# Three Mamba blocks inside one decoder kernel: the skip as a matmul, the gate product on VectorE, one SiLU pass for gate and u

## The reference, cut to what matters

```python
xz = jnp.einsum('bld,ed->ble', h, inproj)
xc, z = jnp.split(xz, 2, axis=-1)
xc = jax.nn.silu(causal_conv(xc, convw, convb))
xdbl = jnp.einsum('ble,fe->blf', xc, xproj)
dt = jax.nn.softplus(jnp.einsum('blr,er->ble', xdbl[..., :R], dtw) + dtb)
A = -jnp.exp(Alog)
# one step of ssm_scan: h = exp(dt*A) * h + (dt*x) * B;  y = sum over 16 states of h * C
y = ssm_scan(dt, Bm, Cm, xc, A) + xc * Dp
y = y * jax.nn.silu(z)
return jnp.einsum('ble,de->bld', y, outproj)
```

## Time and profile before

| | us |
|---|---|
| three runs, median (lowest to highest) | 2925.25 (2921.18 to 2925.6) |
| profiled execution: span from first to last instruction | 2927.1 |
| TensorE busy, of the span | 2456.1 (84%) |
| VectorE busy | 1872.1 (64%) |
| ScalarE busy | 1332.9 (46%) |
| GpSimd busy | 1530.9 (52%) |

### The profile page before, as it was taken

One profiled execution on the slowest core, in us unless ns is written; L12 is line 12 of the kernel. 1 busy time (PEld: TensorE's weight loads), 2 busy tenths in 40 slices (PEclk: granted clock), 3 DMA queues, 4 the chain that ended last, 5 costly groups with the idle time before them and its releaser, 6 DMA issues. The chain is left out here.

```text
span 2927.1 us, 26112 instructions
## 1 busy us (share of the span) xinstructions
PE 2456.1 (84%) x8044; PEld 1106.1 (38%) x8044; DVE 1872.1 (64%) x2521; ACT 1332.9 (46%) x2087; POOL 1530.9 (52%) x1340
## 2 busy tenths in 40 slices
PE   7989989889897788688888549999588989778978
PEld 3333323333332233333333338888332333223322
DVE  2999999999999933466663400000239999994334
ACT  4656466565664433345555212222056565542333
POOL 2999999999999811500000230000439999982010
PEclk9999999999999999899999669999689999999989
DMA  4031230321203000612310324444230320300000
GB/s 186 1 115 47 94 117 1 122 70 55 115 1 115 0 21 17 141 24 33 45 23 1 138 106 181 177 175 175 79 155 1 116 94 24 115 1 20 0 9 29
DMA packets 72193, 215.12 MB, mean 73 GB/s; under 512 B 14044, under 2 KB 39271, under 8 KB 53495
## 3 DMA queue, kind: packets, MB, share of 16 engines
q1 hardware_dynamic: 65380, 180.85, 18.9%
q10 hardware_dynamic: 3602, 24.22, 2.5%
q0 software_dynamic: 3072, 8.39, 0.9%
HBM read 187.80 MB, written 25.43 MB: 73 GB/s over the span
## 5 line engine op out<-in xcount | busy, mean ns | idle before, releaser
L895 POOL TENSOR_TENSOR s_dbu<-s_dx,s_bc 128x512 f32<-128x512 f32 x768 | 967.8, 1284 | 47.9 <-DVE s_psum L561 44.1
L480 PE MATMUL s_psum<-s_hc,ident 128*128 128x512 f32 x1536 | 832.2, 632 | 181.2 <-DVE s_hc L581 170.2
L764 ACT ACTIVATE s_psum<-s_dt,s_a_neg 128x512 f32<-128x512 f32 x768 | 521.6, 688 | 590.5 <-DVE s_hc L581 589.5
L480 PEld LDWEIGHTS s_psum<-s_hc,ident 128*128 128x128 f32 x1536 | 257.9, 192 | 695.2 <-DVE s_hc L581 505.4
L581 DVE TENSOR_TENSOR s_hc<-s_psum,s_bc 128x512 f32<-128x512 f32 x624 | 419.8, 673 | 0.6 <-PE s_psum L480 0.4
L561 DVE TENSOR_TENSOR_SCAN s_psum<-s_psum,s_state,s_dbu 128x512 f32<-128x512 f32 x312 | 395.1, 1277 | 18.5 <-ACT s_psum L764 12.7
L561 DVE TENSOR_TENSOR_SCAN s_psum<-s_psum,s_dbu 128x512 f32<-128x512 f32 x312 | 381.3, 1222 | 22.0 <-ACT s_psum L764 13.8
L1968 ACT ACTIVATE s_probs<-s_banks 128x512 f32<-128x512 f32 (+3 forms) x384 | 169.2, 493 | 149.5 <-PE s_banks L1693 107.0
L2381 POOL DMA_INDIRECT s_rows_in<-moe_out_rows,s_place x32 | 30.6, 957 | 357.0 <-DMA moe_out_rows<-s_ys 347.5
L2360 ACT ACTIVATE s_hidden<-s_banks,s_w 128x256 f32<-128x256 f32 x184 | 77.1, 470 | 300.9 <-PE s_banks L2183 300.9
L163 POOL TENSOR_TENSOR s_pair<-s_res 128x512 f32<-128x512 f32 x4 | 5.0, 1265 | 386.1 <-issue 384.6
(11 more groups left out here) (306 smaller groups left out, 3320.6 us busy)
## 6 DMA issues: line engine op xcount, KB each, us to landing
s_bc<-fwd_rows SPq DMA_DIRECT2D x64, 1024.0 KB, 4.7
s_bc<-m_rows SPq DMA_DIRECT2D x32, 1024.0 KB, 4.7
s_w<-in_moe_w SPq DMA_DIRECT2D x23, 1028.0 KB, 7.2
s_w<-in_moe_w ACTq DMA_DIRECT2D x23, 1024.0 KB, 5.5
qk_parts<-s_parts SPq DMA_DIRECT2D x48, 128.0 KB, 1.9
s_stack_q<-qk_parts SPq DMA_DIRECT2D x48, 128.0 KB, 4.5
s_stack_k<-qk_parts SPq DMA_DIRECT2D x48, 128.0 KB, 7.6
moe_in_rows<-s_zero SPq DMA_DIRECT2D x1, 5888.0 KB, 18.8
```

Source lines behind the costliest of these rows:

```text
L480: pe.matmul(psum[:, SCANS + block_no % 2, :], consts["ident"][:], hc[:, unit % PRODUCTS, :], start=(n == 0), stop=(n == NS - 1)).then_inc( ...
L764: act.activation(psum[:, unit % SCANS, :], dt[:, g % 2, i // NS, :], ACT.Exp, scale=a_neg[CHUNKS[g][0]][:, i:i + 1]).then_inc(decay_ready, 1)
L895: pool.tensor_tensor(dbu[:, unit % TERMS, :], dx[:, g % 2, i // NS, :], bc[:, 2 * n, :], ALU.mult)\
```

## The change

1. The skip is a matmul: `make_skip` (GpSimd) makes diag(D) for each block, and `total` adds skip_in times u as the first matmul of a block's sums, four more per chunk.
2. `skip` and GpSimd's `times_gate` go. VectorE's new `times_gate` reads the sums from PSUM, multiplies by the gate and writes dx, at unit 12 of the next block (the skip stood at unit 3).
3. The gate of a chunk is projected earlier: `in_z` blocks 0, 1, 2 in units 30, 46 and 62 of the chunk before, block 3 in units 16 and 17 of the chunk itself, ahead of `out`, which now begins at 18. ScalarE stores them at units 36 and 51, and 3 and 22. At unit 23 one stretch does SiLU on the gate and on the next u.
4. GpSimd weighs 15 units, i % 16 in (2, 6, 8, 12, 14) of the first three blocks, from two `hs` buffers.
5. Softplus is made in two halves, `dt` has six buffers, and the slots of `rows`, `steps_of`, `var`, `add_res`, `scale_y`, relu and times_u move by one to three units. The table of work banks follows the new order. At the head of each stage the four gate blocks of chunk 0 are projected and copied from PSUM by VectorE (`keep_gate`) between its relu sums.

```diff
-LENT = [i < 3 * NS and i % 4 == 2 for i in range(UNITS)]
+LENT = [i < 3 * NS and i % NS in (2, 6, 8, 12, 14) for i in range(UNITS)]
+GATED, STEPS = 12, 6
-        dt = s.sb("dt", [P, 2, EB, CH])
+        dt = s.sb("dt", [P, STEPS, CH])
-        hs = s.sb("hs", [P, CH])
+        hs = s.sb("hs", [P, 2, CH])
+        skip_in = s.sb("skip_in", [P, EB, P])
...
                 unit = g * UNITS + i
                 block_no, n = unit // NS, unit % NS
                 if n == 0 and block_no >= 2:
-                    pe.wait_ge(y_read, block_no - 1)
+                    pe.wait_ge(y_ready, block_no - 1)
                 elif n == 0:
                     pe.wait_ge(ln_log, block_no + 3)
+                if i == 0:
+                    pe.wait_ge(skip_made, (CHUNKS[g][0] + 1) * EB)
+                if n == 0:
+                    pe.matmul(psum[:, SCANS + block_no % 2, :], skip_in[:, i // NS, :],
+                              u[:, g % 2, i // NS, :], start=True, stop=False)
                 if LENT[i]:
                     pe.wait_ge(product_lent, lent(unit + 1))
                 else:
                     pe.wait_ge(product_ready, own(unit + 1))
                 pe.matmul(psum[:, SCANS + block_no % 2, :], consts["ident"][:], hc[:, unit % PRODUCTS, :],
-                          start=(n == 0), stop=(n == NS - 1)).then_inc(product_used, 1)
+                          start=False, stop=(n == NS - 1)).then_inc(product_used, 1)
...
             variance(2)
             for m in range(EB):
                 for k in range(KD):
+                    in_z(0, m, k)
...
                     total(g, i)
                     if g + 1 < NC and i < 16:
                         conv(g + 1, i // TAPS, i % TAPS)
-                    if g and 16 <= i < 24:
-                        out(g - 1, (i - 16) // EB, i % EB)
-                    if g + 1 < NC and 24 <= i < 28:
-                        rows(g + 1, i - 24)
-                    if g + 1 < NC and i in (30, 31, 34, 35):
-                        steps_of(g + 1, (30, 31, 34, 35).index(i))
-                    if g and post is not None and 36 <= i < 38:
-                        var(g - 1, i - 36)
-                    if i in (38, 39) or 42 <= i < 48:
-                        in_z(g, (38, 42, 44, 46).index(i - i % KD), i % KD)
+                    if g and i in (16, 17):
+                        in_z(g, EB - 1, i - 16)
+                    if g and 18 <= i < 26:
+                        out(g - 1, (i - 18) // EB, (i - 18) % EB)
+                    if g + 1 < NC and 26 <= i < 30:
+                        rows(g + 1, i - 26)
+                    if g + 1 < NC and i in (30, 31):
+                        in_z(g + 1, 0, i - 30)
+                    if g + 1 < NC and i in (32, 33, 36, 37):
+                        steps_of(g + 1, (32, 33, 36, 37).index(i))
+                    if g and post is not None and 38 <= i < 40:
+                        var(g - 1, i - 38)
+                    if g + 1 < NC and i in (46, 47):
+                        in_z(g + 1, 1, i - 46)
                     if g + 2 < NC and 50 <= i < 58:
                         in_x(g + 2, (i - 50) // KD, i % KD)
+                    if g + 1 < NC and i in (62, 63):
+                        in_z(g + 1, 2, i - 62)
...
-            def skip(block_no):
+            def times_gate(block_no):
 
                 g, e = block_no // EB, block_no % EB
                 dve.wait_ge(product_used, NS * (block_no + 1))
-                dve.scalar_tensor_tensor(out=dx[:, g % 2, e, :], in0=u[:, g % 2, e, :],
-                                         scalar=cols[CHUNKS[g][0]][:, 2, e:e + 1], in1=psum[:, SCANS + block_no % 2, :],
-                                         op0=ALU.mult, op1=ALU.add).then_inc(y_read, 1)
+                dve.wait_ge(gate_ready, g + 1)
+                dve.tensor_tensor(dx[:, g % 2, e, :], psum[:, SCANS + block_no % 2, :], gate[:, e, :], ALU.mult)\
+                   .then_inc(y_ready, 1)
+
+            def keep_gate(m):
+                w = tile["gate", 0, m]
+                dve.wait_ge(work_ready[w % 2], w // 2 + 1)
+                dve.tensor_copy(gate[:, m, :], bank(w)).then_inc(work_free[w % 2], 1)
...
-            dve.wait_ge(soft_ready, 1)
+            for m in range(2):
+                keep_gate(m)
             for e in range(EB):
-                dve.tensor_tensor(dt[:, 0, e, :], dt[:, 0, e, :], relu[:, e, :], ALU.add).then_inc(dt_ready, 1)
+                dve.wait_ge(soft_ready, e // 2 + 1)
+                dve.tensor_tensor(step(0, e), step(0, e), relu[:, e, :], ALU.add).then_inc(dt_ready, 1)
                 dve.wait_ge(dt_ready, e + 1)
-                dve.tensor_tensor(dx[:, 0, e, :], dt[:, 0, e, :], u[:, 0, e, :], ALU.mult).then_inc(dx_ready, 1)
+                dve.tensor_tensor(dx[:, 0, e, :], step(0, e), u[:, 0, e, :], ALU.mult).then_inc(dx_ready, 1)
+                if e < 2:
+                    keep_gate(2 + e)
...
-                    if i % NS == 3 and unit >= NS:
-                        skip(unit // NS - 1)
-                    if g and i == 26:
-                        add_res(g - 1, 0)
-                    if g and i == 27:
-                        add_res(g - 1, 1)
-                    if g and post is not None and i == 46:
-                        scale_y(g - 1, 0)
-                    if g and post is not None and i == 47:
-                        scale_y(g - 1, 1)
+                    if i % NS == GATED and unit >= NS:
+                        times_gate(unit // NS - 1)
+                    if g and i in (29, 30):
+                        add_res(g - 1, i - 29)
+                    if g and post is not None and i in (48, 49):
+                        scale_y(g - 1, i - 48)
             weigh(NC * UNITS - 1)
-            skip(NC * EB - 1)
+            times_gate(NC * EB - 1)
...
-                if m == 0 and g >= 2:
-                    act.wait_ge(y_read, EB * (g - 1))
+                if g >= 2:
+                    act.wait_ge(y_ready, EB * (g - 2) + m + 1)
...
 
             def store_gate(g, m):
                 w = tile["gate", g, m]
-                if m == 0 and g:
-                    act.wait_ge(y_ready, EB * g)
+                act.wait_ge(y_ready, EB * (g - 1) + m + 1)
                 act.wait_ge(work_ready[w % 2], w // 2 + 1)
                 act.activation(gate[:, m, :], bank(w), ACT.Copy).then_inc(work_free[w % 2], 1)
 
             def silu_gate(g):
-                for w in (tile["gate", g, EB - 2], tile["gate", g, EB - 1]):
+                for w in (tile["gate", g, m] for m in range(EB)):
                     act.wait_ge(work_free[w % 2], w // 2 + 1)
                 act.activation(gate[:], gate[:], ACT.Silu).then_inc(gate_ready, 1)
 
...
                     if g == 0 and i < EB:
                         store_x(1, i)
+                    if g and i == 3:
+                        store_gate(g, 2)
                     if g + 1 < NC and i in (9, 13, 17, 21):
                         store_conv(g + 1, i // 4 - 2)
-                    if g + 1 < NC and i == 22:
+                    if g and i == 22:
+                        store_gate(g, EB - 1)
+                    if i == 23:
+                        silu_gate(g)
+                    if g + 1 < NC and i == 23:
                         silu_u(g + 1)
-                    if g and post is not None and i == 32:
+                    if g and post is not None and i == 34:
                         square_y(g - 1)
-                    if g + 1 < NC and i == 33:
+                    if g + 1 < NC and i == 35:
                         store_rows(g + 1)
-                    if g + 1 < NC and i in (36, 37, 40, 41):
-                        store_steps(g + 1, (36, 37, 40, 41).index(i))
-                    if g + 1 < NC and i == 42:
+                    if g + 1 < NC and i == 36:
+                        store_gate(g + 1, 0)
+                    if g + 1 < NC and i in (38, 39, 42, 43):
+                        store_steps(g + 1, (38, 39, 42, 43).index(i))
+                    if g + 1 < NC and i == 44:
                         soft_exp(g + 1)
-                    if g and post is not None and i == 44:
+                    if g and post is not None and i == 46:
                         log_var(g - 1)
-                    if g + 1 < NC and i == 44:
+                    if g + 1 < NC and i == 46:
                         soft_log(g + 1)
-                    if g and post is not None and i == 44:
+                    if g and post is not None and i == 46:
                         exp_var(g - 1)
-                    if i in (46, 49, 51, 53):
-                        store_gate(g, (46, 49, 51, 53).index(i))
-                    if i == 55:
-                        silu_gate(g)
+                    if g + 1 < NC and i == 51:
+                        store_gate(g + 1, 1)
                     if g + 2 < NC and i in (57, 59, 61, 63):
...
-            def times_gate(g, e):
-                pool.wait_ge(y_read, EB * g + e + 1)
```

(30 more changed lines are left out.)

86 lines of the change are left out of this document (52 added, 34 removed).

## The result

The changed kernel is slower: 2965.69 us in the median of four runs (2963.00 to 2968.11) beside 2925.43 (2921.18 to 2928.88) of the kernel before on the same chip; ratio 1.0143, 95% interval 1.0130 to 1.0155. The forecast was 2937 in a range of 2918 to 2950. The direction was right and the size was not: +12 forecast, +40 measured. The profiled execution's span is 2964.3 us (2927.1 before).

The account below looks back on a forecast made before the run. VectorE was taken to set the pace, with GpSimd and TensorE having little slack. Chunks +8.1, heads +6.7 and tails -2.8 made +12 on 2925.25: 2937 us, range 2918 to 2950.

Parts of the forecast that it names:

- the path of matmuls: TensorE's 40 matmuls up to the gate's block 3, at 0.858 us each, make scan 24 wait 5.6 us.
- Units 0 to 23: Middle chunks up to scan 24: +2.6 us in a second-half chunk, +2.0 in a first-half one.
- tails: Stage ends: last gating product follows the sums directly, without GpSimd's 1.26 and a hand-over; -2.8 us for two stages.
- units 24 to 63 of the middle chunks: Rest of a middle chunk after scan 24: -0.6 us in a second-half chunk, -1.0 in a first-half one.
- TensorE's lag reaches VectorE: Slower rival, after unit 26: lag outruns four hc buffers, VectorE's weighing waits 1.7 us in eight chunks; 2951, chance 0.12.
- two last chunks: Last chunk of each stage, with one pass as before: -2.2 us each, -4.4 together.
- heads: Stage starts: gate projection and copies delay the relu sums; +3.5 us, and 3.2 in stage 3, together +6.7.
- the weight scaling: Chunk g = 4, a little in g = 2: scaling among GpSimd's gate products moves to 25 and 27; -2.5 us.
- Pass 3.0: First chunk of each stage, no late gate block: the pass costs 3.0 us, within a net +1 each.
- work -2.0: First chunk of each stage: work falls by 2.0 us, within a net +1 each.
- The gate's last block isn't late: Rival at unit 24: TensorE less behind, wait only 3.3 or 3.0 us; 2922, chance 0.20.
- The merged block is covered: Faster rival at unit 23: ScalarE's four decay banks hide the whole SiLU stretch; 2888, chance 0.05.

Follow-up runs that it names:

- no gate pass: The changed kernel with the gate's SiLU run over only one column of each block; ratio 1.0061 to the kernel before.
- add_res earlier: The changed kernel with VectorE's two add_res at units 27 and 28, not 29 and 30; 2964.19 us, ratio 1.0139.
- the split kernel: The changed kernel with block 3's in_z at units 8 and 9, its store at 15, gate SiLU at 18, u's at 22; 2955.76 us, ratio 1.0105.
- the merged one of the same stream: The changed kernel with block 3's in_z at units 8 and 9 and its store at 15, SiLU passes still together; 2968.40 us, ratio 1.0161.
- the kernel with the block at unit 25: The changed kernel with both SiLU passes behind the decay of unit 25, not 23, all stores unmoved; ratio 1.0077.

## Why the prediction was right or wrong

*What held.* The SiLU block was late for the reason given: the path of matmuls puts its wait at 5.6 and it was 5.73 in g = 1; for a first-half chunk 4.4 was forecast, it was 4.29 in g = 6, and units 0 to 23 of g = 6 grew by 1.7 (44.79 against 43.07), where +2.0 stood. **Units 0 to 23** in g = 1: +2.6 forecast, +2.64 measured. In g = 3, 4, 5 and 9 units 0 to 23 last 0.6 to 1.6 more than in their like; there TensorE's granted clock was 0.59 to 0.82 in the chunk's first 4 us, and 1.00 in g = 1, 2, 6 and 10. The pass's second 1.91 us counts in full (no gate pass). The tails gained 1.4 each, -2.8, as forecast.

*The step that failed: units 24 to 63 of the middle chunks.* It read "TensorE's wait there, 0.77, grows to some 2.7, and the stores before the logarithm come 0.6 later: +0.6. Sum -0.6", and for GpSimd "no longer late". The 2.70 came true, and 0.6 is about what the stand itself costs (0.5 by the kernels without a fall of the clock). What the forecast put at nothing is the granted clock behind the stand: 0.57 to 0.66 over 4 us, in each of the eight middle chunks, for 1.7 us each. Measured are +2.06 in g = 1 (77.90 against 75.84) and +0.68 in g = 6, where -0.6 and -1.0 stood. In the kernel without the gate pass the same units of g = 6, with the same stand and the clock at 1.00, last 0.9 less than before: the forecast's -1.0. In g = 1 76.2 is left without the fall, still 1.0 above the forecast's 75.24; 0.6 to 0.9 of that is the wait for GpSimd at scan 43. The eight falls make up some 13 us and the lower clock at the start of four chunks another 4, together 17 of the 28 us by which the forecast was short.

*The rival that came nearest* was "TensorE's lag reaches VectorE". The lag did reach VectorE, but not on the way that the rival names. I let it decide at VectorE's own weighings, which have four buffers of slack, and gave it 0.12; not one of them waited for TensorE. It came through the queues of two other engines: ScalarE's stores, which stand ahead of decays (scans 37 and 40), and GpSimd's weighings, which take turns in the same four buffers and stand ahead of terms that are only three units ahead (scan 43). That its price of 1.7 us a chunk equals that of the clock's fall is luck, and its 2951 is still 14 us short.

*The other terms* (us; the forecast against the difference of the two profiles):

| | forecast | measured |
|---|---|---|
| three second-half middle chunks of stage 0 | +6 | +17.0 |
| three first-half middle chunks of stage 0 | +0.5 | +5.6 |
| two middle chunks of stage 3 | +4 | +11.5 |
| two first chunks | +2 | +6.7 |
| two last chunks | -4.4 | -6.3 |
| heads | +6.7 | +8.4 |
| tails | -2.8 | -2.8 |
| stages 1 and 2, untouched | 0 | -4.6 |
| stages 4 and 5, untouched | 0 | +1.8 |

(The forecast's -2.5 for the weight scaling is in the second row, its +1 for stage 3 in the third.) The scaling of the projection's weights: -2.5 forecast, but g = 4 still has 1.6 us more than g = 6 in units 16 to 23 (19.37 against 17.80). That is the lower clock at its start (0.59), not the scaling: with add_res earlier, where the clock is 1.00 there, units 0 to 23 last 44.79 in g = 4 as in g = 6. The move of the two products gave what was forecast. First chunks: in units 16 to 23 of g = 0 VectorE waits 2.4 for GpSimd, where it waited 1.1; `scale_res` stands there at unit 18, and one weighing more stands just ahead of it. "Pass 3.0" (2.5 measured) was right, "work -2.0" was wrong. Heads: of the 5.06, 1.1 is the later start of the gate's matmuls (58.42, where I let them begin at 57.32), which also differs by up to 6.5 us among kernels with one head. From there to scan 0 the head costs 4.0 in this profile, and 3.5, as forecast, in those where it takes 12.25. In stage 3 it costs 3.35, where 3.2 stood. In g = 3, VectorE waits 1.7 for GpSimd in units 56 to 63, where `make_skip` stands at unit 62; that this is its price is read from the place alone, as no run moved it.

*The rivals that fell.* "The gate's last block isn't late" is refuted by the 3.02 that ScalarE waits for it. "The merged block is covered" is refuted by 5.73. Of the Trainium skill's rule (ScalarE: Activation LUTs, Rules for kernel authors), to run all functions of one table before switching, the split kernel shows the limit: with two loads more per chunk it was 12.6 us faster than the merged one of the same stream. An estimate from the 2.66 us a switch of the same page (What ACT_TABLE_LOAD costs) is 53 us for twenty switches more. A load is 1.28 in the rows, and on ScalarE, busy 69.3 of 125.2 us in a chunk, it costs only what reaches a scan.

*What stays open.* The parts add up to the 37 us between the spans. The -4.6 and +1.8 of the untouched stages are within what profiles of kernels with the same code there differ by: from the last scan of stage 0 to the first of stage 3 they take 1154.6 to 1169.0, and from the last scan of stage 3 to the end 279.4 to 284.1. Why the clock falls behind one stand and not behind an equal one isn't shown, nor how much of the second-half chunks' last 1.0 us is GpSimd's weighings.

## What to carry to other kernels

A change that makes TensorE stand idle can cost more than the stand, since the granted clock may be lower behind it: look at the clock of each chunk, and compare a chunk in which it fell only with another in which it fell. When an engine that runs in order waits, ask what stands behind the waiting instruction and how far ahead its product is, on every engine that shares the buffers, not only on the one that sets the pace; the slack is that of the shortest queue. Merging two blocks that each fit under the work of the others gives one that doesn't, even if it saves their overhead. Where three engines are each busy nine tenths of the time, a gain at one place turns up as a longer instruction or a late term at the next, so cut the chunk at fixed scans and read durations as well as waits before a version is judged by its total.

## What the runs showed of the hardware

- A VectorE instruction with only SBUF operands (`scale_y`, 128x512 in float32) lasted 0.72 to 4.00 us in these kernels, by what GpSimd was doing. Begun 0.09 behind a GpSimd instruction of a back-to-back run it took 3.99 and ended 0.55 behind the run's end; begun half a microsecond into one product it took 1.32 and GpSimd's next product 1.72 instead of 1.27. Scans and weighings, with a PSUM operand, kept 1.22 and 0.67.
- Behind a stand of 2.70 us TensorE's granted clock was 0.65 over the next 4 us in g = 1 of the changed kernel. Behind equal stands it fell in some chunks and not in others: the kernel with the block at unit 25 had 2.91 in g = 1 (0.59) and in g = 3 (1.00). After a wait of 0.61 (add_res earlier, g = 1) it stayed at 1.00.
- The fall made units 32 to 47 1.7 us longer (31.65 against 29.96), through a ScalarE store that stood ahead of a decay.
- ScalarE's table load took 1.28 us and the first activation started 0.01 behind it.
